# Attention cells of a fused decoder: ones' products behind their own wait, a bias product and the bias rows later in the setup

## What is computed

```
x = LN(x + linear attention and MLP(x))            # 16 heads of 16
x = LN(x + banded attention(x, ctx))               # window 128, output bias x_bo
x = LN(x + six cells(x))                           # per cell: 8 heads of 32
    q, k, v = ew[c] * (node @ We + be)
    nodes[c] = act_w[c] * softmax(q Wq (k Wk)^T / sqrt(32)) (v Wv) Wo + q
x = LN(x + causal linear attention(x))
x = LN(x + cross attention(x, ctx, mask))          # output bias y_bo
x = LN(x + real(ifft(fft(x) @ w)) + bias)          # folded into one 256x256 matrix
```

## Time and profile before

| | us |
|---|---|
| median of the runs | 3627.19 |
| the profiled execution, own time | 3627.99 |
| its span | 3626.2 |
| PE busy | 3255.1 (90%) |
| DVE busy | 2274.6 (63%) |
| ACT busy | 1710.2 (47%) |
| POOL busy | 1021.0 (28%) |

### The profile page before, as it was taken

One profiled execution on the slowest core, in us unless ns is written; L12 is line 12 of the kernel. 1 busy time (PEld: TensorE's weight loads), 2 busy tenths in 40 slices (PEclk: granted clock), 3 DMA queues, 4 the chain that ended last, 5 costly groups with the idle time before them and its releaser, 6 DMA issues.

```text
span 3626.2 us, 77617 instructions
## 1 busy us (share of the span) xinstructions
PE 3255.1 (90%) x31500; PEld 2413.5 (67%) x31500; DVE 2274.6 (63%) x4093; ACT 1710.2 (47%) x3465; POOL 1021.0 (28%) x795
## 2 busy tenths in 40 slices
PE   6898998998898999999999999999999999998875
PEld 5676766676676767766676776667677666766654
DVE  5666458557567486757666675767667576465633
ACT  1244454454455445454545545454554545544532
POOL 5865006005024153315051331505033150000000
PEclk8999999999999999999999999999999999999987
DMA  6110100010100101011010101101010110100000
GB/s 218 60 53 22 56 22 16 22 45 16 42 28 28 39 13 51 25 31 33 23 42 19 48 25 31 33 22 42 19 48 25 31 33 16 30 16 13 13 7 4
DMA packets 123132, 122.88 MB, mean 34 GB/s; under 512 B 9760, under 2 KB 122656, under 8 KB 122656
## 3 DMA queue, kind: packets, MB, share of 16 engines
q1 hardware_dynamic: 122784, 117.91, 11.0%
HBM read 113.69 MB, written 4.19 MB: 33 GB/s over the span
## 4 chain that ended last, share of the span: by engine, by line
PE 61%; DVE 13%; ACT 9%; POOL 8%; issue 7%; DMA 1%; SPq 0%; DVEq 0%; POOLq 0%; ACTq 0%
PE banks L721 16%; PE banks L713 13%; PE banks L896 7%; PE banks L925 6%; PE banks L871 6%; DVE nmx L1228 5%; POOL work L1609 5%; ACT work L1461 4%; POOL work L1619 3%; PE banks L706 2%; PE banks L882 2%; PE banks L728 2%; PE banks L931 2%; PE banks L900 2%; PE banks L1003 1%
## 5 line engine op out<-in xcount | busy, mean ns | idle before, releaser
L1228 DVE TENSOR_REDUCE nmx<-banks 128x4 f32<-128x1024 f32 (+1 forms) x640 | 720.5, 1165 | 279.3 <-PE banks L871 277.3
L721 PE MATMUL banks<-work,weights 128*128 128x256 f32 x3584 | 864.4, 390 | 33.9 <-DVE work L1251 17.6
L721 PEld LDWEIGHTS banks<-work,weights 128*128 128x128 f32 x3584 | 674.9, 194 | 169.6 <-issue 53.8
L1461 ACT ACTIVATE work<-banks 128x1024 f32<-128x1024 f32 (+1 forms) x640 | 596.7, 980 | 302.9 <-PE banks L900 301.0
L713 PE MATMUL banks<-weights,work 128*128 128x256 f32 x2688 | 661.0, 392 | 40.0 <-ACT work L1461 14.6
L713 PEld LDWEIGHTS banks<-weights,work 128*128 128x128 f32 x2688 | 505.5, 195 | 141.6 <-issue 47.7
L1619 POOL TENSOR_TENSOR work<-work 128x512 f32<-128x512 f32 x256 | 405.1, 1601 | 183.2 <-DVE work L1198 121.6
L896 PE MATMUL banks<-work 32*128 32x256 f32 (+1 forms) x5120 | 401.2, 400 | 44.6 <-issue 19.8
L871 PE MATMUL banks<-work 32*128 32x256 f32 (+1 forms) x5120 | 354.8, 394 | 41.9 <-DVE nmx L1228 15.2
L1652 POOL TENSOR_TENSOR work<-work,row 128x512 f32<-128x512 f32 x64 | 87.6, 1368 | 995.2 <-PE banks L706 995.2
L1245 DVE TENSOR_TENSOR added<-work 128x1024 f32<-128x1024 f32 x192 | 254.4, 1326 | 180.1 <-ACT work L1461 169.8
(11 more groups left out here) (156 smaller groups left out, 3525.9 us busy)
## 6 DMA issues: line engine op xcount, KB each, us to landing
weights<-in_w_all SPq DMA_DIRECT2D x322, 256.0 KB, 2.7
work<-in_w_setup SPq DMA_DIRECT2D x41, 256.0 KB, 4.8
work<-in_ctx SPq DMA_DIRECT2D x32, 256.0 KB, 3.0
work<-in_x SPq DMA_DIRECT2D x16, 256.0 KB, 2.9
out<-work SPq DMA_DIRECT2D x16, 256.0 KB, 2.2
weights<-in_w_all SPq DMA_DIRECT2D x1, 3072.0 KB, 15.8
row<-in_rows SPq DMA_DIRECT2D x1, 1664.0 KB, 7.3
mrow<-in_mask SPq DMA_DIRECT2D x16, 32.0 KB, 3.6
```

The costliest lines, as they stand in the source:

```text
L721: ins = e.matmul(b[:, m * 256:m * 256 + 256], wslot(w)[:, k, m * P:m * P + P], xin[:, k, :], start=(k == 0 and (m == 0 or closed)) if star ...
L1228: e.tensor_reduce(nmax(s, n)[:, 2 * p:2 * p + 2, :], b, AX, ALU.max, negate=True).then_inc(*freed("max", n, p, i))
L1461: e.activation(dst, src, ACT.Exp).then_inc(*freed("exp", n, p, i))
```

## The change

The bias product gets a need, the last Fourier step; the rows get a semaphore of their own and are issued behind the six operands of node 2; those that read rows wait for it once; and the wait for `added` stands between the values' and the ones' products.

```diff
-    folded("ob", 0, 3.8, "DVE", 0.8)
+    folded("ob", 0, 3.8, "DVE", 0.8, ("PE", "four", 2))
...
+        in_rows = signal("s_loaded_rows", 16)
...
                     if kind == "c":
-                        e.wait_ge(*when("added", a, i))
                         e.wait_ge(*when("cv", c, i))
...
                     if kind == "c":
+                        e.wait_ge(*when("added", a, i))
                         for g in range(4):
                             ins = e.matmul(b[32 * g:32 * g + 32, S:2 * S], ones[:, 0:32], added[:, half, g, :],
...
-            e.dma_start(row[:, :, :].rearrange("p r n -> p (r n)"), rows.partition_broadcast(P)).then_inc(
-                *tell(in_vec, "vectors"))
...
                     for n in NODE_LOADS:
                         operand(f"{n}{a}", in_node[a], "node operands", a)
+                    if a == 2:
+                        e.dma_start(row[:, :, :].rearrange("p r n -> p (r n)"), rows.partition_broadcast(P)).then_inc(
+                            *tell(in_rows, "rows"))
```

More of the change, by code:

```diff
@@ L542, in build @@
         stored = [signal(f"s_stored{s}", 16) for s in range(NS)]
-        signals = ([setup_pe, setup_vec, setup_act, setup_pool, in_vec, in_fourier] + list(in_w.values()) + in_ring + in_node + evicted
+        signals = ([setup_pe, setup_vec, setup_act, setup_pool, in_vec, in_rows, in_fourier] + list(in_w.values()) + in_ring + in_node + evicted
                    + pe + vec + act + pool + in_x + in_ctx + in_mask + stored)
@@ L1118, in vector @@
                     e.wait_ge(*when("ob mm"))
+                    once("rows")
                     for j, n in enumerate(("x_bo", "y_bo")):
```

## The result

| | before | after |
|---|---|---|
| median of the runs, us | 3627.59 (6 runs, 3625.88 to 3637.21) | 3601.56 (6 runs, 3595.57 to 3603.26) |
| ratio of the runs | | 0.9923, 95% interval 0.9913 to 0.9934 |
| the profiled execution, own time and span | 3627.99, 3626.2 | 3601.38, 3599.7 |

The change takes off 26 us, where 11.5 were forecast. The time lies in the range given (3600 to 3638) and outside the forecast's own range (3608 to 3620).

A forecast was written before the change was run, and what follows sets the result against it. The matmuls were taken to bound the long middle, after a startup of some 1600 us. Terms -9.2 + 2.6 - 4.9 = -11.5 gave 3615.7 us, range 3600 to 3638, the forecast's own range 3608 to 3620.

The forecast's parts named there:

- Leaving the front: First 31 us: without the bias product, loads issue by about 13 us; all priorities stay; no separate size in the sum.
- the luck can fall the other way: Startup: a new order with shorter startup intervals, down to some 3600 us; chance 0.07.
- the same cycle is the natural end: Stores after 1594.88: unchanged priorities and older entries first lead back to the same cycle; argument against a slower order.
- The rows: First projection's eviction waits for the rows, landing at 21.7 us instead of starting at 30.94: -9.2 us, bounds -10.9 and -3.8.
- The new place: Bias product behind the last Fourier product near 151.56 us: 1.9 plus 0.7 for its eviction, +2.6 us, bounds 0 and +10.0.
- The wait: Values' products of 192 outputs no longer wait for VectorE's add: -4.9 us, bounds 0 and -8.7.
- Its price: Ones' weight loads now carry a wait, mostly long met: counted as 0 apiece.
- No worth: Rival: gaps closed by the wait's move come back as others, 3620.6 us; 0.15 together with the early start lost.
- Slower, first: Rival: planner settles into another cycle after 1594.88, ten entries at 213.7 us, +23, 3638.7 us; chance 0.19.
- Slower, second: Rival: the mid-stream wait costs 0.12 us at each of 192 outputs, +23, 3638.7 us; chance 0.04.

The follow-up runs named there:

- new order alone: Planner run over the change's needs, then bias product and its streams put back to the front; rows and wait as before: 3615.34 us, 0.9970.
- the rows sooner: The changed kernel with the rows' load issued ahead of node 2's operands instead of behind: 3600.44 us, 0.9935.
- the old order: Kernel before's order kept, bias product behind the last Fourier product, rows late, wait as before: 3623.92 us, 0.9994; first added bias six steps later: 3622.69, 0.9992.
- the whole change with `fold` 1.9: The changed kernel with the planner's assumed time of a fold step 1.9 instead of 1.8: 3600.81 us, 0.9924.
- `fold` 1.9 alone: The kernel before with only the planner's assumed time of a fold step 1.9 instead of 1.8: 3600.00 us, 0.9916.
- one other number: The kernel before with the planner's assumed time of `n5` 1.0 instead of 1.2: 3691.48 us, 1.0177.
- one other Fourier step as the need: The changed kernel with the bias product's need set to the Fourier step before the last: 3667.58 us, 1.0106.
- the rows alone: The kernel before with only the rows' part of the diff; bias product at the front, order and wait as before: 3636.22 us, 1.0020.
- after again: The changed kernel run once more, unchanged, beside the run with the rows' load issued earlier: 3600.57 us, 0.9933.
- the wait alone: The kernel before with only the wait for `added` moved between the values' and the ones' products: 3627.04 us, 0.9993.

## Why the prediction was right or wrong

**Leaving the front: the step that failed.** "All priorities stay as they are; only the product's place in time moves." The priorities did stay. But a list scheduler with a place less in its first steps picks another ready step at once, and from there all picks differ: the last Fourier product came 19.5 us earlier, entry 2's MLP output 72 us. The new order got 0 in the sum. By the run of the new order alone it is the largest single term: ratio 0.9970 (0.9959 to 0.9980), 11 us. The prediction had the mechanism as a rival ("the luck can fall the other way", 0.07) and gave its worse side 0.19, though the profile had no row to tell the sides apart. Its argument "the same cycle is the natural end" held for the cycle; it said nothing about the way there, and that is where orders differ.

**The rows: right in kind, 2.1 us less, and not simply carried on.** Forecast eviction 21.7, measured 23.84, so -7.1 instead of -9.2. The product was done at 21.96 instead of near 20.0. The first entry's statistics were there 2.1 us sooner, as forecast (from 10.93 instead of 13.05), yet its normalization began at 15.17 instead of 15.26: ScalarE now had the eviction of the context's transpose in front of its part, with a table load of 1.28 us at 11.40, and a second load at 13.31. The sum left that queue out. The rows landed 2.1 us later than the mean rate said. The bytes came as forecast, 5.9 MB from 4 to 22 us; then the transfers ran thin (kernel after, 0 to 40 us, tenths of busy share and GB/s per microsecond):

```profile
DMA  0023697899989999999994182079988999999999
GB/s 0 11 28 45 132 324 192 244 364 364 349 288 311 359 366 356 348 432 433 435 413 200 53 183 79 0 172 362 235 247 273 358 377 375 360 354 342 352 347 346
```

In the slices that begin at 21 and 22 us the 16 DMA engines are busy to 4 tenths and to 1 tenth and move 200 and 53 GB/s, while the rows are still on their way until 23.8. A mean rate leaves out this tail. These 2 us do not matter: with the rows sooner the eviction comes at 21.98 and the time stays. That the start is carried to the end one to one is what did not hold. In the old order it was gone by the sixth store; in the new order the product's place and the rows' place brought 0.9970 to 0.9945, 9 us; and the whole change with `fold` 1.9, a new draw again, was no faster than `fold` 1.9 alone.

**The new place: right near its low end in the new order.** Product 1.89, eviction 0.74, and no idle time ahead of the product, so no stream in the way (its price of 2.8 for a landing stands in no row; the page's median is 2.7); the planner did put other pieces first on POOL, and the added bias runs 1.4 us after the bias's eviction begins, 4.0 us later than before. The term left out was the bank: the mask products waited 0.47 for the eviction. In the old order POOL's stand was real: 2.81 us of the bound of 10.0.

**The wait: gaps right, worth wrong.** About 17 outputs close behind an add, and 8.7 us to be had. With the order held, the idle time ahead of the values' products fell from 33.1 to 22.0 us and 2.3 came back ahead of the ones' (old order), and from 37.3 to 23.7 with 1.6 back (new order). That exceeds the 4.9 taken. But in the old order nothing of it was left in the time. In the cycle the move takes 3.5 us of idle time from seven entries, and the busy time of the same matmuls rises by 4.3. In the new order and with `fold` 1.9 the ratios are 0.0006 to 0.0022 lower with the move (2 to 8 us), each time inside overlapping intervals. "No worth" was thus right for the old order; for the others a few us are possible and not shown.

**Its price: right.** From the start of the last values' product to the first ones' product it is 196 ns at the median both before and after; after, 184 of the 192 outputs lie at 195 to 197, and five of the other eight begin 0.06 us behind the end of an add. So a met wait on the ones' weight load cost nothing that can be measured. The Trainium skill (Perfetto Trace Analysis, Per-engine timelines) says that the matmul queue can pull weight loads ahead of running matmuls; these rows show no price for a met wait on such a load, and they do not show whether loads were pulled ahead. What unmet waits cost is the 1.6 us.

**Slower, first: not here, but near.** The mechanism exists, and its price was set too low: with one other number, or one other Fourier step as the need, the plan enters the cycle only at entry 11 or 10, and the time rises by 64 or 38 us against before, not by 23. **Slower, second** did not occur.

Sums: forecast -9.2 + 2.6 - 4.9 = -11.5. Measured, along one path of kernels and by their ratios: order -11, product's place -4, rows' place -5, wait -4 to -8 (from 0.9945 to 0.9933, 0.9932 or 0.9923), together -24 to -28. Each but the first has an uncertainty of some 5 us, since the intervals of neighbours overlap, so none of the three is shown by itself, and the shares hold for this path only: in the old order the parts gave 0, and the rows alone +7.

What stays open: why one startup order leaves 165 and another 148 us of gaps, and why the same matmuls take 1430 us in the one and 1417 in the other, with 113 and 82 us at the clock's lower level. No single wait was found that makes it; the gaps are spread over 1600 us, and no run holds the clock while the order changes.

## What to carry to other kernels

Where a list scheduler writes the order, an edit to one need or one assumed time is a new draw of the whole startup, and the draw (here -30 to +64 us for one number that touches no computation) can be larger than what the edit saves. So hold the order fixed by hand and apply the edit, and take the new order and put the edited steps back; only the two together say what the edit is worth. Compare the written plans too: two kernels that differ in a planner's number can be the same program. Judge a startup by the time at which the cycle begins, split into idle and busy time of the bound engine, not by the first store; and before a gap on a nearly full matmul engine is counted as a gain, look at the busy time of the same matmuls after it has gone.

## What the runs showed of the hardware that was not expected

**Closed gaps can come back as slower matmuls.** In the cycle the granted clock is at its upper level (2.4 GHz) but for one short stretch at about the same place of most entries, where it is near half (1.2 GHz). Windows and timeline of the whole change with `fold` 1.9 about two such places, 423 us (two entries) apart:

```profile
1866.00:1873.00 7.00, 5.74 (x49) 4.25 (x47) 6.96 (x10) 2.04 (x5) 5.42 (x4) 1.00 0.12 37
1873.00:1880.00 7.00, 5.91 (x34) 4.45 (x35) 5.60 (x10) 3.03 (x6) 1.52 (x1) 0.53 0.01 2
1880.00:1887.00 7.00, 7.00 (x101) 4.21 (x99) 6.27 (x9) 4.34 (x8) 1.27 (x1) 0.98 0.13 40
...
2296.00:2303.00 7.00, 6.07 (x35) 4.61 (x36) 5.59 (x10) 3.03 (x6) 1.50 (x1) 0.55 0.01 2
```

```profile
1861.86 1.89 PE L722 MATMUL banks<-work,weights 128*128 128x256 f32 x8
...
1874.09 1.23 PE L897 MATMUL banks<-work 32*128 32x256 f32 x8 [1.60 <-issue]
...
1877.44 3.31 PE L722 MATMUL banks<-work,weights 128*128 128x256 f32 x8
```

The engine has idled 0.74 and 1.60 us just there, and the eight products of L722 take 3.31 us instead of 1.89. From the sixth to the thirteenth store, eight profiled executions with the old wait and orders that have reached the cycle had 27 to 38 us at the lower level, 109.7 to 112.7 us idle, and took 1478.1 to 1480.2 us. Seven with the moved wait had 106.3 to 107.9 idle, and 44 to 48 us at the lower level in six of them, which took 1479.3 to 1481.2; the seventh is the profiled execution of after, with 27 us and 1474.8. So 5 of the 26 us between the two profiled executions of before and after come from where the clock happened to be low, and are not work saved; after again had its cycle in 1481.2. This is one execution of each kernel. Over all runs the mean granted clock is 0.9687 with the wait alone (12 runs) against 0.9698 for before beside it (28 runs), which points the same way; in the new order (0.9736 with the old wait, 0.9732 to 0.9738 with the moved one) and with `fold` 1.9 (0.9740 in both) it does not move. So that the clock takes back closed gaps is seen in the cycle of these traces and not shown as a rule, and what makes it fall was not tested.

**The spread of one kernel.** With the order of before, single executions of the same kernel lay between 3615 and 3640 us. Four to twelve runs of each gave intervals 0.2 to 0.45% of the time wide, and each part of the change is 0.1 to 0.3%.
